# Attention numerator and denominator taken transposed in column tiles, and the expert's low-rank product in row tiles, in a two-layer kernel on one core

## The reference, cut to what matters

```
# layer 0, token mixing: kernelised attention, 16 heads of 8, 32 features a head
xp = einsum(x * norm, proj); diag = 0.5 * norm^2 * sum(x^2)
stab = max over features (queries) | max over tokens and features of a head (keys)
qp, kp = ratio * (exp(xp - diag - stab) + 1e-4)
out = einsum(qp, ctx) / einsum(qp, k_sum)        # ctx = kp^T v, k_sum = sum of kp
x1 = layer_norm(h + out @ Wo.T + bo); y = layer_norm(x1 + relu(x1 @ W1.T + b1) @ W2.T + b2)
# layer 0, feed-forward: 8 experts with a shared base and a low-rank part (rank 4)
inter = relu(x @ wi.T + wi_b + (x @ A[e].T) @ B[e].T)   # e = argmax of the gate
out = inter @ wo.T + wo_b
# layer 1, token mixing: a test-time-trained linear state W per head (16 heads of 64),
# updated chunk by chunk of 64 tokens; then a receptance-weighted channel mix
```

## Time and profile before

| | us |
|---|---|
| median of 3 runs | 1056.03 (1055.14 to 1057.24) |
| the profiled execution, its own time | 1055.22 |
| its span, first to last instruction | 1053.4 |
| TensorE matmul busy (share of the span) | 987.2 (94%) |
| VectorE busy | 811.9 (77%) |
| ScalarE busy | 658.3 (62%) |
| GpSimd busy | 345.2 (33%) |
| layer 0 of pair 0 alone | 0 to about 161.6 |
| three periods | about 161.6 to 869 |
| slots of the last pair alone | about 869 to 1053.4 |

### The profile page before, as it was taken

How to read it: one execution, slowest core, us unless ns; L and a number is a source line. 1 busy time by engine, 2 the same in 40 slices (tenths; PEclk the granted TensorE clock), 3 DMA queues, 4 the chain that set the end, 5 groups by cost and what they waited for, 6 DMA issues and landing times.

```text
span 1053.4 us, 27018 instructions
## 1 busy us (share of the span) xinstructions
PE 987.2 (94%) x10968; PEld 754.9 (72%) x10968; DVE 811.9 (77%) x1977; ACT 658.3 (62%) x1244; POOL 345.2 (33%) x399
## 2 busy tenths in 40 slices
PE   6869989999999999999999999999999999899994
PEld 5458556678878776578879776588879776577773
DVE  2983636996879878996779878997778875888873
ACT  2423226586775566688675566689685566676773
POOL 0980001141434232132334142133434132436542
PEclk9968998998999999999999999999999998999997
DMA  9000000000000010000000010000000000000000
GB/s 329 1 1 2 1 21 21 2 2 2 1 2 2 2 41 12 1 2 2 2 2 12 1 42 12 2 1 2 2 2 12 2 21 12 1 2 12 2 2 21
DMA packets 15833, 16.16 MB, mean 15 GB/s; under 512 B 2014, under 2 KB 14302, under 8 KB 15326
## 3 DMA queue, kind: packets, MB, share of 16 engines
q1 hardware_dynamic: 15709, 14.43, 4.5%
HBM read 10.23 MB, written 2.10 MB: 12 GB/s over the span
## 4 chain that ended last, share of the span: by engine, by line
PE 65%; DVE 20%; ACT 6%; issue 4%; POOL 3%; DMA 0%; DVEq 0%; POOLq 0%; ACTq 0%; SPq 0%
PE ps L537 9%; PE ps L590 5%; PE ps L530 4%; PE ps L573 4%; PE ps L612 4%; PE ps L596 3%; PE ps L584 3%; PE ps L458 3%; PE ps L481 3%; PE ps L490 3%; PE ps L412 3%; PE ps L519 2%; POOL gbase L1268 2%; PE ps L511 2%; DVE tmp L1076 2%
## 5 line engine op out<-in xcount | busy, mean ns | idle before, releaser
L1268 POOL TENSOR_TENSOR gbase<-zhat,gamma 128x512 f32<-128x512 f32 x64 | 83.3, 1302 | 432.9 <-DVE scl L1065 425.6
L1276 POOL TENSOR_TENSOR zq_sqq<-zq_sqq,qinv 128x512 f32<-128x512 f32 x64 | 68.4, 1077 | 186.2 <-DVE qinv L1088 181.6
L756 ACT COPY w_sb<-ps 65x1024 f32<-65x1024 f32 x72 | 72.6, 1008 | 18.8 <-PE ps L590 15.4
L590 PEld LDWEIGHTS ps<-grad,k_sc 64*65 64x65 f32 x2048 | 67.7, 138 | 22.8 <-issue 18.2
L590 PE MATMUL ps<-grad,k_sc 64*65 64x64 f32 x2048 | 76.0, 225 | 5.0 <-DVE grad L1082 4.7
L537 PEld LDWEIGHTS ps<-w_sb,keys 65*64 65x64 f32 x2048 | 66.1, 139 | 19.9 <-issue 15.7
L537 PEld LDWEIGHTS ps<-w_sb,queries 65*64 65x64 f32 x2048 | 65.7, 139 | 16.1 <-issue 4.8
L537 PE MATMUL ps<-w_sb,keys 65*64 65x64 f32 x2048 | 73.7, 226 | 3.6 <-ACT keys L764 2.4
L537 PE MATMUL ps<-w_sb,queries 65*64 65x64 f32 x2048 | 73.1, 225 | 1.5 <-issue 0.8
L596 PE MATMUL ps<-h,pack_ttt 128*128 128x128 f32 x512 | 71.1, 284 | 2.2 <-ACT tiles L692 1.3
L573 PE MATMUL ps<-pack_ttt,h 128*128 128x512 f32 x128 | 71.9, 650 | 0.0
(11 more groups left out here) (241 smaller groups left out, 2455.0 us busy)
## 6 DMA issues: line engine op xcount, KB each, us to landing
x<-in_x SPq DMA_DIRECT2D x8, 256.0 KB, 3.0
xc<-x SPq DMA_DIRECT2D x16, 128.0 KB, 2.4
out_x<-xc SPq DMA_DIRECT2D x16, 128.0 KB, 2.4
pack_ttt<-in_ttt SPq DMA_DIRECT2D x1, 1216.0 KB
w_sb<-in_compose SPq DMA_DIRECT2D x1, 1024.0 KB, 7.4
keys<-in_gam_bet_rows SPq DMA_DIRECT2D x1, 1024.0 KB
pack_expert<-in_expert SPq DMA_DIRECT2D x1, 792.0 KB, 11.9
zq_sqq<-in_wmod SPq DMA_DIRECT2D x1, 768.0 KB, 4.2
```

Of the source, the lines that this page charges most:

```text
L590: last = mm(bank[2 * f + c][0:C, h * HD:(h + 1) * HD], k_sc[64 * c:64 * c + 64, HH * f + h, :], grad[64 * c:64 * c + 64, h, :], start=Fals ...
L756: nc.scalar.copy(w_sb[:, f, :, :, :].rearrange("p b h d -> p (b h d)"), ps[0:C, 2 * f:2 * f + 2, :].rearrange("p a c -> p (a c)")).then_in ...
L1268: P.tensor_tensor(gbase[:, cols], zhat[:, cols], gamma2[:, cols], ALU.mult).then_inc(S["g_hat"], 1)
L1276: P.tensor_tensor(heads(zq_hat[:, cols]), heads(zq_hat[:, cols]), per_head(qinv[:, hs]), ALU.mult).then_inc(S["zq_ready"], 1)
```

## The change

ATTEND now takes the 32-column blocks of the context as stationary operands and streams the 512 tokens of the query features past them, four groups at partitions 32g: once for the denominators (each repeated 8 times) and once for the numerators. ScalarE copies both. ATTN_T transposes the denominators back to tokens in partitions, VectorE takes the reciprocals and spreads them; a new step ATTN_N transposes these again, and VectorE multiplies them with the numerators. K_SHIFT adds the stabiliser to all four tiles by one matmul of 64 columns. The gate rows come from transposes. The mask and the product `um` are formed for four copies of the 32 low-rank columns, `lora_b` has its four blocks in partitions 32f, and EXPERT1 issues two `wi` matmuls and then two low-rank ones with K = 32 each, in two banks. Several tiles share storage. All orders and `BANKS` are new.

```diff
-    "expert": [..., ("lora_b", FF), ("first", E)],
+    "expert": [..., ("lora_b", 128), ("first", E)],
...
     "PE": (
-        ("r0ksnkl1sa01qlbq0akn0dklb1aedl1eab1k0bdqnlfkefqlad0qbe1aobkf0lkdq1aeqdf1lbokn1ea1d1b0qkl10feadl10qf0bkae0o0b1d"
-          "fklqbfaed1klqlead0obb0am0kkfedflqqoeam0d10fq0lbkf01ae01qdm1bl0oead1b1fqdfene10offmo1m"),
+        ("r01ksnklsa0l1qb0akq0ndlb1keadl1qeba1fnk0dbkflel0qadqbe1akk0ofbldq1aeqdf1bon0lk11ea1b1kqdl0fae1ld10bqf00aed01o0"
+          "kblffqbaedk1lbkqaed0kol0flma0edfkqb0aemo10qqf0kld1fbea0lo0db1mnq01aed1qfb1dfee1of0fmo1m"),
...
-                ctx=sb(f"ctx{u}", [128, G, 36]), y=...
+                ctx=sb(f"ctx{u}", [128, 2, G, 32]), y=...
-                um=sb(f"um{u}", [128, T, E * R]), umT=sb(f"umT{u}", [128, N]),
+                um=tiles[:, 2, :]..., umT=tiles[:, 3, :], eqr=sb(f"eqr{u}", [128, T, E, R]),
+            L[u]["numT"] = tiles[:, 0, :]
...  TensorE
-                        last = mm(bank[b][:, k * D:(k + 1) * D], mod_all[...].broadcast_to([128, 128]),
-                                  ident, start=True, stop=True)
+                        last = nc.tensor.transpose(bank[b][:, k * D:(k + 1) * D], mod_all[...].broadcast_to([128, 128]), ident[:, :])
...  K_SHIFT
-                    for t in range(T):
-                        o = bank[b][:, t * H0:(t + 1) * H0]
-                        mm(o, l["k2"][:, t * 128:(t + 1) * 128], half_square[:, :], start=True, stop=False)
-                        last = mm(o, ones[0:H0, :], l["sd"][:, :], start=False, stop=True)
+                    mm(bank[b][:, 0:T * H0], ones[0:H0, :], l["sd"][:, :].unsqueeze(1).broadcast_to([H0, T, H0]), start=True, stop=False)
+                    for t in range(T):
+                        last = mm(bank[b][:, t * H0:(t + 1) * H0], l["k2"][:, t * 128:(t + 1) * 128], half_square[:, :], start=False, stop=(t == T - 1))
...  ATTEND
-                    for half in range(2):
-                        b = begin(f"num{u}{half}_{p}")
-                        for t in (2 * half, 2 * half + 1):
-                            for g in range(G):
-                                at = (t % 2) * 256 + 36 * g
-                                last = mm(bank[b][:, at:at + 36], l["qf"][:, g, t * 128:(t + 1) * 128], l["ctx"][:, g, :], start=True, stop=True)
+                    for n, name in ((1, "den"), (0, "num")):
+                        b = begin(f"{name}{u}_{p}")
+                        for g in range(G):
+                            last = mm(bank[b][32 * g:32 * g + 32, :], l["ctx"][:, n, g, :], l["qf"][:, g, :], start=True, stop=True)
                         end(last, b)
                 elif step == ATTN_T:
-                    b = begin(f"attnT{u}_{p}")
+                    b = begin(f"denT{u}_{p}")
+                    ready(f"den{u}_{p}")
                     for t in range(T):
                         last = nc.tensor.transpose(bank[b][:, t * 128:(t + 1) * 128], l["y"][:, t, :], ident[:, :])
+                elif step == ATTN_N:
+                    b = begin(f"rden{u}_{p}")
+                    ready(f"denT{u}_{p}")
+                    for t in range(T):
+                        last = nc.tensor.transpose(bank[b][:, t * 128:(t + 1) * 128], l["qT"][:, t * 128:(t + 1) * 128], ident[:, :])
...  EXPERT1
-                    for f in range(NF):
-                        b = begin(f"f2{u}{f}_{p}")
-                        mm(bank[b], w_i[:, f * 128:(f + 1) * 128], l["hT"][:, :], start=True, stop=False)
-                        end(mm(bank[b], lora_b[:, f * 128:(f + 1) * 128], l["umT"][:, :], start=False, stop=True), b)
+                    for together in ((0, 1), (2, 3)):
+                        into = []
+                        for f in together:
+                            b = begin(f"f2{u}{f}_{p}")
+                            into.append(b)
+                            mm(bank[b], w_i[:, f * 128:(f + 1) * 128], l["hT"][:, :], start=True, stop=False)
+                        for f, b in zip(together, into):
+                            er = slice(E * R * f, E * R * (f + 1))
+                            end(mm(bank[b], lora_b[er, :], l["umT"][er, :], start=False, stop=True), b)
...  ScalarE
-                    nc.scalar.copy(l["ctx"][:, :, 0:32], ...)
-                    nc.scalar.copy(l["ctx"][:, :, 32:36], ...).then_inc(drained(f"ctxT{u}_{p}"), 1)
+                    nc.scalar.copy(l["ctx"][:, :, :, :].rearrange("p n g d -> p (n g d)"), src[:, 0:256]).then_inc(drained(f"ctxT{u}_{p}"), 1)
-                elif step == ATTN_T:
-                    nc.scalar.copy(l["q2"][:, :], src).then_inc(drained(f"attnT{u}_{p}"), 1)
+                elif step == ATTEND:
+                    src = filled(act, f"den{u}_{p}")
+                    nc.scalar.copy(l["y"][:, :, :].rearrange("p t d -> p (t d)"), src).then_inc(drained(f"den{u}_{p}"), 1)
+                    filled(act, f"num{u}_{p}")
+                    nc.scalar.copy(l["numT"], bank[fills[f"num{u}_{p}"][0]]).then_inc(drained(f"num{u}_{p}"), 1)
...  VectorE
-                elif step == ATTEND:
-                    (two reciprocals of 128x32, four products of 128x128)
+                elif step == ATTN_T:
+                    src = filled(dve, f"denT{u}_{p}").rearrange("p (t h e) -> p t h e", t=T, e=DH)
+                    link(V.reciprocal(l["rden"][:, :, :], src[:, :, :, 0]))
+                    V.tensor_copy(l["qT"]..., l["rden"]... .broadcast_to([128, T * H0, DH])).then_inc(drained(f"denT{u}_{p}"), 1)
+                elif step == ATTN_N:
+                    src = filled(dve, f"rden{u}_{p}")
+                    ready(dve, f"num{u}_{p}")
+                    V.tensor_tensor(l["q2"][:, :], l["numT"], src, ALU.mult).then_inc(drained(f"rden{u}_{p}"), 1)
                     biased[u] = go_on(V.tensor_tensor(x[:, u, :, :], x[:, u, :, :], over(gg3[:, u, 1, :], T), ALU.add))
...  GATE
-                    link(V.tensor_tensor(eq, eq, lm... .broadcast_to([128, T, E]), ALU.is_equal))
-                    V.tensor_tensor(l["um"]... , src... , eq... .broadcast_to([128, T, E, R]), ALU.mult)
+                    link(V.tensor_tensor(each[:, :, :, :], eq... , lm... .broadcast_to([128, T, E, R]), ALU.is_equal))
+                    V.tensor_tensor(l["um"]... , src... .broadcast_to([128, T, NF, E * R]), each... .broadcast_to([128, T, NF, E * R]), ALU.mult)
...  GpSimd
-            for t in (L[0]["umT"][:, :], L[1]["umT"][:, :]):
-                then(P.memset(t, 0.0))
```

More of the change, by code:

```diff
@@ L68 @@
     "attn2": [("ctx_mask", 128), ("wo0", D), ("w1", FF), ("w2", NF * D)],
-    "expert": [("gate_a", GA), ("wi", FF), ("wof", NF * D), ("lora_b", FF), ("first", E)],
+    "expert": [("gate_a", GA), ("wi", FF), ("wof", NF * D), ("lora_b", 128), ("first", E)],
     "ttt": [("wk1", HW), ("wq1", HW), ("w_r", D), ("w_kf", D), ("w_vf", D)],
@@ L89, in shape_constants @@
     }
-(LN1_STATS, LN1, QKV, Q_SHIFT, K_MAX, STABLE, K_SHIFT, K_FEATURES, CONTEXT, Q_FEATURES, ATTEND, ATTN_T, PROJECT, LN2, FF1, FF2,
- LN3, LN4, GATE, LORA, EXPERT1, EXPERT2, LN5, N_STEPS) = range(24)
+(LN1_STATS, LN1, QKV, Q_SHIFT, K_MAX, STABLE, K_SHIFT, K_FEATURES, CONTEXT, Q_FEATURES, ATTEND, ATTN_T, ATTN_N, PROJECT, LN2, FF1, FF2,
+ LN3, LN4, GATE, LORA, EXPERT1, EXPERT2, LN5, N_STEPS) = range(25)
 (MIX_STATS, MIX_NORM, MIX_SHIFT, MIX_IN, MIX_OUT, N_MIX) = range(6)
@@ L124 @@
[L124 to L131 removed]
+        ("zzzyyzzyozyzzoyyzyyzozzoyyzyzyzyzyooyyoo"),
@@ L312, in build @@
         LEVELS = HD.bit_length() - 1
-        N_LAYER0_SET = 6
+        N_LAYER0_SET = 4
         N_POOL_SET = N_LAYER0_SET + 4 + 10 + 1 + LEVELS + LEVELS + 1 + 1 + 5 + 1 + 2
@@ L398, in layer0 @@
                     for k in range(2):
-                        last = mm(bank[b][:, k * D:(k + 1) * D], mod_all[:, 2 + 3 * k, 2 * p + u:2 * p + u + 1].broadcast_to([128, 128]),
-                                  ident, start=True, stop=True)
+                        last = nc.tensor.transpose(bank[b][:, k * D:(k + 1) * D], mod_all[:, 2 + 3 * k, 2 * p + u:2 * p + u + 1].broadcast_to([128, 128]),
+                                                   ident[:, :])
                     end(last, b)
@@ L466, in layer0 @@
                     end(last, b)
+                elif step == ATTN_N:
[3 more added lines that the diff above has]
+                        last = nc.tensor.transpose(bank[b][:, t * 128:(t + 1) * 128], l["qT"][:, t * 128:(t + 1) * 128], ident[:, :])
+                    end(last, b)
                 elif step == PROJECT:
                     b = begin(f"y1{u}_{p}")
-                    ready(f"attnT{u}_{p}")
+                    ready(f"rden{u}_{p}")
                     for t in range(T):
@@ L504, in layer0 @@
                     for t in range(T):
-                        last = nc.tensor.transpose(bank[b][0:E * R, t * 128:(t + 1) * 128], l["um"][:, t, :], ident[:, :])
+                        last = nc.tensor.transpose(bank[b][:, t * 128:(t + 1) * 128], l["um"][:, t, :], ident[:, :])
                     end(last, b)
@@ L740, in layer0 @@
```

(2 more changed lines are left out.)

76 lines of the change are left out of this document (33 added, 43 removed).

## The result

The changed kernel takes 1046.87 us (median of 17 runs, 1044.96 to 1053.22) against 1055.14 for the kernel before, run between them (median of 17, 1046.64 to 1061.81): ratio 0.9938, 95% interval 0.9914 to 0.9962. So it is 0.6% faster. That is 8.3 us by the medians and 6.5 by the ratio, a third or less of the 24.7 foreseen, and outside the stated range of 1020 to 1044. A few executions, of the unchanged kernel too, ran far slower (the slowest 3340 us), and the ratios leave them out. The profiled execution took 1053.22 us, 6.3 above the median of its kernel; what its trace says of totals has to be read with that.

The account below looks back on a forecast made before the run. TensorE's own work was taken to bound the periods. Saving 3.7 us a sequence gave 22 there, less 2.8 made 19; with 5.7 in the first part, 24.7 off 1055.2 gave 1030.5, stated as 1031; range 1020 to 1044.

Parts of the forecast that it names:

- ATTEND: Attention on TensorE: four overlapping column tiles cut 3.60 us to 2.03, saving 1.6 a sequence.
- ATTN_N: New attention step on TensorE: adds four transposes, 0.47 us, leaving a net attention saving of 1.1 a sequence.
- K_SHIFT: Key shift on TensorE: fewer instructions and changes of tile shape cut 2.48 us to 1.25, saving 1.2 a sequence.
- EXPERT1: Expert step on TensorE: low-rank matmuls in two-fold overlapping row-tile pairs cut 6.86 us to 5.6, saving 1.2 a sequence.
- (b): Rival for the tiles in attention and expert step: they overlap only two-fold, giving 1055 us; chance 0.03.
- (c): Rival for the expert step: row tiles do not overlap, it saves nothing and pays 0.48, giving 1045 us; chance 0.06.
- (d): Rival for attention: column tiles take turns at 512 columns, costing 7.1 us a sequence, giving 1072 us; chance 0.03.
- the conversion: In the periods, a TensorE microsecond saved is worth up to one; 22 us saved, 2.8 let be lost, leaves 19.
- rival (a): In the periods VectorE or the longer chain becomes the limit; half the gain is lost, 1040 us; chance 0.22.
- The first part: Start of the run, before the periods: 2.1 + 2.2 + 2.4 - 1.0 = 5.7 us saved.
- The last part: End of the run, without layer 0: its new order taken at 0, within 2 us either way.
- the three longer hops: Attention result's longer chain before PROJECT: nothing counted, as other work covers it; each uncovered hop would cost 0.7 to 1.3.

Follow-up runs that it names:

- the added maxima: K_MAX's four maxima on VectorE taken twice, 21.6 us in all: 1072.79 us in the changed kernel, 1082.38 us in the kernel before.
- the PSUM version: Changed kernel with K_SHIFT's four VectorE subtractions reading the shift from PSUM instead of a copy in SBUF: 1040.78 us, ratio 0.990.

## Why the prediction was off

**K_SHIFT, ATTEND, EXPERT1: right.** Priced at 1.25, 2.03 and 5.6 us, they cost 1.27, 1.86 and 5.84; ATTN_N was priced at 0.47 and costs 0.49. Together they save 1.21 + (3.60 - 1.86 - 0.49) + 1.02 = 3.5 us a sequence where 3.5 was foreseen, gates aside. Rivals (b), (c) and (d) are out: the column tiles overlap about four-fold at 512 columns too (16 instructions in 1.86 us, with two changes of shape, where one alone takes 0.429), and four low-rank instructions in row-tile pairs take 1.05 us where four alone would take 1.72.

By the 3.07-fold of the Trainium skill's page "TensorE: Matmul & The Clock Gate" (section "Measured speedup vs the span model") ATTEND was estimated at 2.5 us; this trace disagrees, by 0.6 us.

**The failed step is the conversion: "so a microsecond of TensorE saved in a period is worth up to a microsecond", with VectorE's added work "costed at nothing".** The prediction took the 86% of the stretch with slots alone as a share that VectorE can have without setting the pace, and an average of 87% over a period as no more than that. The runs show that VectorE set the pace beside TensorE already in the kernel before: in its periods about 16 us more of VectorE's work cost 24.3, and 15.4 more of TensorE's cost 14.9. The kernel was balanced, its chain passing from one engine to the other, for 26.5 us at a time off TensorE. When one of two balanced engines gets faster, the other is left. In the changed kernel TensorE's next microseconds are worth nothing to half (old K_SHIFT back: 0 to 3 for 9.7; 17 us of low-rank work out: 0; 20.5 more: 8.6), and added VectorE work still costs more than itself (21.6: 26). It is rival (a), priced at a loss of 9.5 us; the loss was 16.4.

**Its size.** VectorE's 15 us more in the periods, at the 27 / 21.6 = 1.25 of the added maxima, would be 19 us, near the 16.4 that are missing. That is an estimate, and the two are not shown to be the same microseconds; the PSUM version, where less than half of the VectorE time came back, speaks against so high a price for every one of them. Of the 15, some 2 are own work: GATE costs the 0.5 a sequence that was priced, but the copy into 512 columns takes 0.43 us undisturbed and not 0.69. The rest is the same work made longer by GpSimd beside it, which the prediction could not see in a duration averaged over the group: the 931 ns of the subtractions before were already a mixture of 0.68 and more.

**The first part: nearly right.** -4.0 in the profiled execution for -5.7 foreseen. K_SHIFT alone gives 5.9 there in the kernel before, where 2.1 was foreseen for it; so the gains there do not add either, and that the total came near is in part luck.

**The last part: 0 foreseen, 4.7 us longer in the profiled execution,** at a granted clock of 0.89 instead of 0.94. Much of this is that execution's own, as 179.7 to 184.2 us in six of the eight variants with the same last part show.

**The clock.** TensorE's granted clock has two levels here, 1.2 and 2.4 GHz. In the profiled execution of the changed kernel four stretches within the periods are at the lower one for 6.8 to 10.3 us, and each begins within 1 us of the end of a wait for VectorE of over a microsecond: for `gbase` behind the second K_SHIFT of each period, and once for `grad` behind EXPERT1. The second period (the wait, then columns as in the earlier trace rows):

```profile
467.05 1.98 PE L545 MATMUL ps<-w_sb,keys 65*64 65x64 f32 x32 [1.12 <-DVE gbase L1078]
```

```profile
466.00:468.00 2.00, 0.95 (x18) 0.95 (x20) 1.97 (x4) 1.44 (x2) 0.46 (x1) 0.65 0.00 0
468.00:470.00 2.00, 2.00 (x44) 2.00 (x41) 1.93 (x4) 1.24 (x3) 0.00 (x0) 0.50 0.00 0
```

Over all runs the time at the lower level can be worked out as 2 x (1 - clock) x span. Within one kernel it goes with the span, mostly by 0.3 to 0.5 us for each of these us (0.23 in the changed kernel itself; correlation mostly 0.8 to 0.98). Its median is 86 us before and 93 after, so some 2 to 3 of the 16.4 missing microseconds. In the variants of the changed kernel it rises as TensorE's work falls against VectorE's: 76 with 20.5 us more of TensorE, 78 with the low-rank matmuls one at a time, 90 with the old K_SHIFT, 93 in the changed kernel as it is, 105 without the low-rank matmuls, 114 with more VectorE work, and 71 to 77 in the variants that relieve VectorE. So a part of what TensorE saves is lost again at the lower level, by these slopes an estimated 4 to 6 us of the 17 in the run without low-rank matmuls, and a part of added work comes back, an estimated 5 to 8 us of the 20.5. The order of these medians is measured; that waits for VectorE bring the level down is read from where the stretches lie and was not tested by itself.

**Open.** How much of the missing time is VectorE's priced additions, how much GpSimd's neighbourhood, how much the lower clock level, and how much the three longer hops of the attention result. The orders and `BANKS` could not be tried without the new attention form, whose steps they contain, so what they are worth by themselves was not measured.

## What to carry to other kernels

Before converting an engine's saved microseconds into time, ask what the second engine would do with them: its share of the chain that ended last (20% here, with 26.5 us at a stretch), and one run with its work increased, say more than its busy share of 83%. Then ask in which part of the run an edit gained, since two kernels with equal gains can have them in different parts. In a balanced kernel, take work from both engines or expect less; here it was a third. And read durations by what ran beside them: a group whose mean is 931 ns where its size takes 680 has a neighbour that a new order will move.

## What the hardware showed beyond that

- An fp32 subtraction of 512 columns on VectorE with both inputs in SBUF takes 0.68 us alone and 1.31 on average beside GpSimd, at most 2.54; beside a GpSimd memset it stays at 0.68; with one input in PSUM all 32 took 0.669 to 0.689. A 128-column fp32 TENSOR_SCALAR from SBUF to SBUF takes 0.34 us, and the six that began beside GpSimd's multiplications of 512 columns took 1.19 on average.
- GpSimd's multiplication of 128x512 takes 1.71 us beside such a subtraction, against a median of 1.27.
- Four column tiles with 512 fp32 columns each cost 0.116 us an instruction, changes of shape included, against 0.429 for one on the full array; four-fold overlap would be 0.107 and leaves 0.14 us for the two changes.
- Two row tiles of K = 32 with 512 columns: four instructions in 1.05 us, for 0.86 if the overlap were complete and the changes of shape free.
